# Graph attention over edges on one core: turned one-hots from streamed destination numbers, the other one-hots on GpSimd, eight groups per loop turn

## What is computed

```python
# logx: (H=4, n, DH=64); s_i, s_j: (n, 4)
alpha = leaky_relu(s_i[dst] + s_j[src], 0.2)
m     = segment_max(alpha, dst)
a     = exp(alpha - m[dst])
ssum  = segment_sum(a, dst)                  # a is later divided by ssum[dst]
out   = segment_sum(logx[:, src] * a, dst)   # per head, 64 features
```

## Time and profile before

| | |
|---|---|
| time, median of 3 runs | 9486.06 us (9477.93 to 9505.69) |
| the profiled execution's own time | 9485.6 us |
| its span | 9483.6 us |
| busy: PE, DVE, ACT, POOL | 43%, 42%, 19%, 54% |
| the stretch of `attend`'s groups | about 6972 to 7942 us of the span |

### The profile page before, as it was taken

One profiled execution on the slowest core, in us unless ns is written; L12 is line 12 of the kernel. 1 busy time (PEld: TensorE's weight loads), 2 busy tenths in 40 slices (PEclk: granted clock), 3 DMA queues, 4 the chain that ended last, 5 costly groups with the idle time before them and its releaser, 6 DMA issues. The chain is left out here.

```text
span 9483.6 us, 78659 instructions
## 1 busy us (share of the span) xinstructions
PE 4045.1 (43%) x14501; PEld 2859.4 (30%) x14502; DVE 3947.4 (42%) x8209; ACT 1803.0 (19%) x6789; POOL 5163.3 (54%) x5240
## 2 busy tenths in 40 slices
PE   4000035555476676875454410000046663845444
PEld 2000024444355555433333300000034552333332
DVE  5000023333355555432222367777776666222223
ACT  0000001111100000220000014444446663100000
POOL 5777756666666666126666407777721110166665
PEclk7555567677788888986666655555578887967666
DMA  3000012222255555233333315555553333333334
GB/s 101 3 14 6 3 61 87 88 87 88 102 173 172 171 174 172 48 140 91 92 91 90 71 49 179 180 179 177 178 124 113 115 113 92 134 89 92 91 90 86
DMA packets 390541, 997.00 MB, mean 105 GB/s; under 512 B 133180, under 2 KB 167648, under 8 KB 383836
## 3 DMA queue, kind: packets, MB, share of 16 engines
q0 software_dynamic: 227264, 559.12, 21.0%
q1 hardware_dynamic: 163228, 437.33, 14.0%
HBM read 684.30 MB, written 311.78 MB: 105 GB/s over the span
## 5 line engine op out<-in xcount | busy, mean ns | idle before, releaser
L797 POOL DMA_INDIRECT rel_rows<-relation_rows,rel_ring_row x1664 | 1612.8, 969 | 1400.0 <-ACT rel_ring_end L781 903.2
L809 PE MATMUL rel_sums<-rel_rows,rel_hot 128*128 128x256 f32 x3328 | 1199.9, 505 | 1235.8 <-issue 705.5
L809 PEld LDWEIGHTS rel_sums<-rel_rows,rel_hot 128*128 128x128 f32 x3328 | 817.1, 253 | 1619.5 <-issue 1428.7
L1635 POOL DMA_INDIRECT nmax_rows<-messages,nmax_ring_row x832 | 878.2, 1056 | 653.6 <-ACT nmax_ring_row L1582 393.4
L621 POOL DMA_INDIRECT rows_by_src<-spread_rows,spread_ring_place x832 | 814.0, 978 | 488.3 <-issue 244.6
L694 POOL DMA_INDIRECT both_rows<-batch_normed,both_ring_row x832 | 816.6, 982 | 458.6 <-issue 232.7
L488 POOL DMA_INDIRECT records_by_dst<-sort_ring_rec,sort_ring_place x784 | 836.5, 1067 | 293.1 <-issue 234.5
L599 PE MATMUL spread_p_r<-g_big,spread_hot_t 128*128 x1664 | 632.0, 546 | 561.5 <-ACT spread_hot_t L543 397.7
L833 DVE TENSOR_TENSOR g_acc<-rel_sums,g_acc 128x256 f32 x832 | 351.2, 422 | 1209.1 <-remote 581.8
L706 PE MATMUL both_out_sums<-both_out_rows,both_out_hot 128*128 128x257 f32 x1664 | 515.8, 465 | 405.0 <-DVEq L743 378.4
L1818 PE MATMUL att_sums<-att_weighted,att_hot 128*128 128x260 f32 x1664 | 542.3, 482 | 312.4 <-DVE att_weighted L1888 169.9
(11 more groups left out here) (384 smaller groups left out, 6784.1 us busy)
## 6 DMA issues: line engine op xcount, KB each, us to landing
both_out_rows<-rows_by_src SPq DMA_DIRECT2D x208, 520.0 KB
kept_rows<-nmax_rows SPq DMA_DIRECT2D x208, 520.0 KB
att_rows<-kept_rows SPq DMA_DIRECT2D x208, 520.0 KB
rel_rows<-relation_rows,rel_ring_row POOLq DMA_INDIRECT x1664
relation_rows<-mix_table SPq DMA_DIRECT2D x25, 1024.0 KB
relation_rows<-rel_table SPq DMA_DIRECT2D x25, 1024.0 KB
rows_by_src<-spread_rows,spread_ring_place POOLq DMA_INDIRECT x832
both_rows<-batch_normed,both_ring_row POOLq DMA_INDIRECT x832
```

The costliest lines, as they stand in the source:

```text
L797: pool.indirect_dma_start(rows[:, j, 0:words], None, table, bass.IndirectOffsetOnAxis(ap=ring_row[:, j:j + 1], axis=0)).then_inc(landed[r] ...
L809: last = nc.tensor.matmul(sums[:, 2 * r + q // 2, 0:width], hot[:, j, :], rows[:, j, :], start=q % 2 == 0, stop=q % 2 == 1)
L1635: pool.indirect_dma_start(rows[:, j, :], None, msg_dram.ap(), bass.IndirectOffsetOnAxis(ap=ring_row[:, j:j + 1], axis=0)).then_inc(landed[ ...
```

## The change

1. The local numbers of all edges are also written to DRAM in edge order, as bf16 (`local_of_edge`, 832 x 128). `neighbour_max` makes them before its loop: seven transposes on PE, three copies on ACT, two small stores on SP.
2. `attend` streams them back to all partitions: one DMA puts the 2048 numbers of 16 columns (four groups) on each of the 128 partitions, 512 KB. VectorE compares the whole of it with the partition's own number (`g.own`): one instruction, 128x2048 in bf16, gives the turned one-hots of four groups. The transposes on PE, the copies on ACT and the bf16 one-hots are gone.
3. GpSimd makes the float32 one-hots itself: four comparisons of 128x128 per group, `g.iota` against the edge's number, 832 in all, written out without a loop. The only wait is that the sums of group n-4 are done.
4. A loop turn has eight groups (TURN = 8), so 26 turns; each loads 16 tile numbers at once where it loaded 8.

```diff
+            stream_locals(0, 0)
             for r in range(RING):
                 stream(0, r)
+            stream_locals(0, 1)
...
+            with sp.Fori(1, TURNS) as i:
+                for r in range(TURN):
+                    if r % RING == 1:
+                        sp.wait_ge(turned_ready, i * 2 + (r // RING - 1))
+                        stream_locals(i, r // RING)
+                    sp.wait_ge(ready, i * TURN + (r + 1 - RING))
+                    sp.wait_ge(shared, i * TURN + (r + 1 - RING))
                     stream(i, r)
```

```diff
+            def stream_locals(i, u):
+                sp.dma_start(local_row[:, u, :], local_at[bass.ds(i * (2 * WIDE * P) + u * (WIDE * P), WIDE * P)]
+                             .partition_broadcast(P)).then_inc(local_in[u], 16)
```

```diff
-                nc.gpsimd.tensor_copy(hot[:, s, :], hot_b[:, s, :]).then_inc(widened, 1)
...
+            for n in range(CH // GRP):
+                pool.wait_ge(summed, n + 1)
+                for q in range(GRP):
+                    last = nc.gpsimd.tensor_scalar(hot[:, n % RING * GRP + q, :], g.iota[:],
+                                                   g.rec[0][:, n * GRP + q, 2:3], None, ALU.is_equal)
+                last.then_inc(hot_ready, 1)
```

```diff
+            def build(i, u):
+                dve.wait_ge(local_in[u % 2], (i + u // 2) * 16 + 16)
+                nc.vector.tensor_scalar(hot_t[:, u % 2, :], local_row[:, u % 2, :], g.own[:], None,
+                                        ALU.is_equal).then_inc(turned_ready, 1)
...
-                    if not (last_turn and r == RING - 1):
-                        more = not (last_turn and r >= RING - 3)
-                        scores(i, r + 1, (lambda: build(i, r + 3)) if more else None)
+                    if not (last_turn and r == TURN - 1):
+                        scores(i, r + 1)
+                    if r % RING == 0 and not (last_turn and r == RING):
+                        build(i, r // RING + 1)
                     if not (first and r == 0):
                         before = tiles[2 * r:2 * r + 2]
```

More of the change, by code:

```diff
@@ L1639, in _ @@
         def _(pe):
+            for k in range(STRIPS):
+                count = min(P, CH - k * P)
+                last = nc.tensor.transpose(p_l[0:count, k, :], g.rec[0][:, k * P:k * P + count, 2], g.ident[:])
+            last.then_inc(local_turn, 1)
             for t in range(T):
@@ L1720, in attend @@
         sums = m.ps("sums", [P, 4, 512])
-        p_t = m.ps("p_t", [P, 2, 2 * GRP, P], BF16)
         p_s = m.ps("p_s", [P, 2, 512])
-        (tick, shared, hot_ready, widened, turn, back, looked, alphas, exps, ready, summed, added, vec, psum_free) = (
-            m.sem(n) for n in ("tick", "shared", "hot_ready", "widened", "turn", "back", "looked", "alphas", "exps", "ready",
+        (shared, hot_ready, turned_ready, looked, alphas, exps, ready, summed, added, vec, psum_free) = (
+            m.sem(n) for n in ("shared", "hot_ready", "turned_ready", "looked", "alphas", "exps", "ready",
                                "summed", "added", "vec", "psum_free"))
         landed = [m.sem(f"landed_{r}") for r in range(RING)]
+        local_in = [m.sem(f"local_in_{u}") for u in range(2)]
         own_in = m.sem("own_in")
@@ L1749, in _ @@
         def _(pool):
[L1750 to L1759 removed]
+            for n in range(CH // GRP):
[4 more added lines that the diff above has]
+                last.then_inc(hot_ready, 1)
         @block.scalar
         def _(act):
[L1763 to L1773 removed]
+            with act.Fori(0, TURNS) as i:
+                for r in range(TURN):
+                    at = r % RING * GRP
+                    act.wait_ge(alphas, i * TURN + (r + 1))
+                    act.wait_ge(summed, i * TURN + (r + 1))
+                    nc.scalar.activation(weighted[:, at:at + GRP, D:W], alpha[:, r % 2, :, :],
                                          ACT.Exp).then_inc(exps, 1)
[L1775 to L1776 removed]
+                    act.wait_ge(exps, i * TURN + (r + 1))
+                    for q in range(at + GRP - SHARE, at + GRP):
                         for h in range(H):
@@ L1863, in then @@
                     c.wait()
-                c.step(nc.vector.tensor_reduce(
+                then(nc.vector.tensor_reduce(
                     seen[:].rearrange("p q s -> p (q s)"),
                     p_s[:, r % 2, 0:PARTS * GRP].rearrange("p (s n) -> p s n", n=3), AX.X, ALU.add))
-                if more:
-                    more()
-                c.wait()
                 then(nc.vector.tensor_tensor(al, rows[:, at:at + GRP, D:W], seen[:, :, 0:H], ALU.add))
@@ L2048, in build @@
         hyperbolic_prepare(nc, g, a, lx_dram, msg_dram)
-        neighbour_max(nc, g, msg_dram, kept_dram)
+        neighbour_max(nc, g, msg_dram, kept_dram, local_dram)
         clear(nc, (g.acc[:],))
-        attend(nc, g, kept_dram, msg_dram)
+        attend(nc, g, kept_dram, local_dram, msg_dram)
         hyperbolic_finish(nc, g, a, o_dram)
```

158 lines of the change are left out of this document (71 added, 87 removed).

## The result

The changed kernel takes 9575.4 us (median of 4 runs, 9567.47 to 9582.93), the kernel before 9488.84 (4 runs, 9477.93 to 9505.69): ratio 1.0086, 95% interval 1.007 to 1.0102, so 66 to 97 us slower. The profiled execution took 9567.47 us, its span is 9565.5.

What follows compares the result with a forecast made beforehand. A chain of waits, not one engine, was taken to bound `attend`. The terms summed to 20.52 us per four groups, 1059 us for the stage against 970, plus 3 before the loop: 9578 us, range 9468 to 9690.

Steps and rivals of the forecast that it cites:

- four groups: DVE's chain in `attend`: a group falls from 3.91 to 3.10 us, so four take 12.40.
- GpSimd beside DVE: GpSimd's comparisons, about 0.30 us each, delay DVE by one instruction per meeting: 1.10 us per four groups.
- wait and wide comparison: DVE's wait for the streamed numbers, 3.80 us, plus its wide comparison, 0.80 us, per four groups.
- TensorE's clock: After idling during the wait, PE runs its next sums slowly and delays the look-up: 1.20 us per four groups.
- loop turn: Half as many turns, with sixteen tile numbers costing no more than eight: 1.22 us per four groups, from 2.45.
- The scores get shorter: On DVE, alpha's first step starts 0.48 us sooner and its last step is 0.33 us shorter, per group.
- The wide comparison: DVE's bf16 comparison of 2048 elements per partition takes 0.80 us, bounds 0.70 and 2.3.
- The wait: Numbers issued behind rows on SP land 4.65 us after the multiplications' end; DVE waits 3.80 us, 50 times.
- rival 2: The streamed numbers land before DVE needs them, so no wait: 838 us for `attend`, 9357 in all; chance 0.09.
- rival 1: The wait stays, GpSimd costs nothing: 9521 us, or 9474 if the DMA also overlaps better; chance 0.27.
- rival 3: DVE stays blocked through all four GpSimd comparisons, 2.6 us for 1.10 per four groups: 9656 us; chance 0.18.

Runs made afterwards that it cites:

- e1_early: The changed kernel with the streamed numbers for each wide comparison issued four groups earlier on SP; 8482.95 us, ratio 0.985 to the kernel before.
- e7_quarter: e1_early with one of GpSimd's four comparisons per group (all four in the first four groups only); ratio 0.982 to the kernel before.
- e3_poolcmp: The kernel before with only GpSimd's copy replaced by the four float32 comparisons; 8569.86 us, ratio 0.9949.
- e5_spread: e1_early with tile numbers loaded two at a time, behind the multiplications on VectorE and ahead of each look on TensorE; 9180.47 us, ratio 0.9756.
- e10_plain: The kernel before with GpSimd's copy replaced by four comparisons and tile numbers loaded two at a time, without streamed numbers; 8487.46 us, ratio 0.9859.

## Why the prediction was right, and where two errors cancelled

Direction, size (+87 us measured, +92 predicted) and the central mechanism held. Per four groups, the turn printed above gives 40.71 / 2 = 20.36 us against 20.52. The terms:

| term | predicted | measured |
|---|---|---|
| four groups | 12.40 | 12.40 (taken over) |
| GpSimd beside DVE | 1.10 | 0.35 |
| wait and wide comparison | 3.80 + 0.80 | 4.59 |
| TensorE's clock | 1.20 | 0.91 |
| loop turn | 1.22 | 2.12 |
| sum | 20.52 | 20.37 |

"Measured" comes from the rows of the timeline: the turn is 4.37 less the 0.14 of an ordinary place, halved; the clock is (0.94 + 0.87) / 2; wait and comparison are the time from the end of alpha to the additions, 7500.36 to 7505.37, less the 0.41 gap that stands there in other groups (4.60, and 4.58 for the second). What is left of 40.71 is 25.49, or 12.75 per four groups; 12.40 is taken as forecast and 0.35 given to GpSimd. That is an upper limit: by the instructions that get longer beside GpSimd in the changed kernel's trace (139 multiplications by 21 ns, 130 last steps of alpha by 36, 26 wide comparisons by 66) it is 9 us, 0.2 per four groups.

- **The scores get shorter: right.** The first step of alpha starts 0.28 us behind the reduction, and the last takes 0.17 to 0.23; undisturbed groups take 3.11 to 3.14.
- **The wide comparison: right**, 753 ns by the median of its 52, 786 by the mean. It is nearer to my 0.80 than to the Trainium skill's 693 ns ("VectorE: DVE Perf Modes", "The perf-mode tier table"), which it exceeds by 60.
- **The wait: right in kind, a little short.** Rows issued at m + 0.17 (m = 7499.57), numbers 0.52 behind them, data on the way until about 7504.2 = m + 4.6, as forecast. The comparison starts only at m + 5.09: some 0.5 us pass after the last data. It comes 50 times in the loop, as forecast. e1_early shows that the wait, and not the comparison or the bytes, is what the change lost by. The prediction's rival 2, the numbers in time, gave 838 us for the stage; e1_early's stretch is 813.
- **TensorE's clock: right**, 0.9 in place of 1.2: sums at 3.81 and 3.70 behind each wait, then the look-up is late by 0.94 and 0.87.
- **The loop turn: wrong.** The step that failed is "sixteen tile numbers per load cost no more than eight, by the loop that already loads 16". The gap grew from 2.59 to 4.37, so halving the turns saved 131.5 - 110.0 = 21.5 us, not 64. What went wrong is told below: the row came from a loop whose load of 16 is a cheaper one, 0.42 us in the very turn of the earlier trace rows, against 3.60 here.
- **GpSimd beside DVE: wrong twice, in opposite directions.** The comparison was estimated at 0.30 us from a select; it takes 0.60 (median). The meeting with DVE was priced as a full wait for one instruction, by the copy's example; e7_quarter shows 19 us for three quarters of them, and in e3_poolcmp alpha's last step is not held at all. The size of the term is at most 0.35 and not 1.10, 39 us over the stage.

The two errors, 0.90 too little and 0.75 too much, cancelled by luck; without it the forecast would have been off by some 40 to 47 us, still within the range. Rivals 1 and 3 asked what GpSimd costs: rival 1, with nothing, was nearer to it than the forecast, and still gave too low a time, 9521, since its loop turn was as wrong.

The rule behind rival 3 stands on the page "SBUF — State Buffer", section "Who interferes with whom" of the Trainium skill: whoever issues first has the shared ports for a whole instruction. It describes the copy (0.50 us in place of 0.18), and not these comparisons, which take 600 ns: the step of alpha stays at 175 ns beside them in e3_poolcmp, and where it is held, in e1_early, it takes 231 ns by the median and 286 at most. The measurement decides here. Why the copy holds DVE to its end, and a comparison only for a small part of its time, no run here shows.

## What to carry to other kernels

When a new transfer feeds a step on the critical engine, look for the instruction in whose shadow it is issued: here it stood in the queue behind a wait that is met when the engine already wants the data, and the same transfer issued four groups earlier turned a loss of 0.9% into a gain of 1.5%. Price loads of registers by their own rows, and not by the gap of another loop, and put them behind running work in small pieces: worth 75 to 82 us of the stretch in each of the three kernels in which it was tried (against 964.3 on chip A for the kernel before). And count idle time on TensorE twice: behind its idle time of 3.8 us the sums of the next group took 3.81 us, where they take 1.99 at full clock.

## What the runs showed of the hardware

**Loads of tile numbers.** The profile has a row for them, which the prediction did not read. First the changed kernel in `attend`, 16 numbers (by line: count, then ns as min/median/max; DVEq and PEldq are the engines' sequencers):

```profile
L928 PEldq TENSOR_LOAD <-g_pair_tile x27: 555/3805/3835, 6961.0 to 7984.0; - x27
L928 DVEq TENSOR_LOAD <-g_pair_tile x27: 525/3604/3622, 6968.6 to 8020.0; - x27
```

The kernel before in three stages: `neighbour_max` (8 numbers from 8 i on), `attend` (8 from 8 i - 2 on), and the second `aggregate` (16 from 16 i on):

```profile
L926 DVEq TENSOR_LOAD <-g_pair_tile x61: 594/606/1721, 5007.8 to 6911.2; - x61
...
L926 DVEq TENSOR_LOAD <-g_pair_tile x53: 526/1845/1849, 6973.2 to 7939.9; - x53
...
L926 DVEq TENSOR_LOAD <-g_pair_tile x26: 5/1097/1114, 8233.9 to 9426.9; - x26
```

and e5_spread, 2 numbers:

```profile
L928 PEldq TENSOR_LOAD <-g_pair_tile x208: 532/537/570, 6890.7 to 7631.5; - x104
L928 DVEq TENSOR_LOAD <-g_pair_tile x208: 523/529/549, 6901.9 to 7638.4; - x104
```

In `attend`, 2, 8 and 16 numbers take 0.53, 1.85 and 3.60 us: 0.22 us for each more. The Trainium skill ("Runtime: NRT & Kernel Launch", "Instruction fetch mechanics") puts a load of registers at about 200 ns for each, speaking of those that the runtime puts in; the rows of `attend` come near it. The other two stages don't: 8 numbers take 0.60 us there and 16 take 1.10, a third as long. The loop of the earlier trace rows, the first `aggregate`, has such loads too; in the turn from which the failed step of the prediction was read it took 0.42 us:

```profile
L926 DVEq TENSOR_LOAD <-g_pair_tile x1: 418/418/418, 4723.7 to 4723.7; - x1
```

The visible difference is where the first number stands, at a multiple of the count or two off it. TensorE's loads in an early stage (1289 to 2454 us of the span) fit this: 24 numbers from 24 i on, 1.74 us by the median of 17, where 16 take it 3.80 in `attend`. That this is the cause is a guess, and was not tried.

**The queue runs ahead.** A load of 0.53 us behind two multiplications leaves next to no gap on DVE (e5_spread): with 208 of them in place of 26 loads of 3.60 us, the idle time ahead of the multiplications falls by 95 us, and that ahead of the reduction stays at 14.9, with 1.0 of "issue".

**GpSimd.** A comparison with a number per partition, 128x128 in float32, takes 590 ns at least, twice a select of that size; the four of one group, at 7503.57, took 2.84 us. Beside DVE both sides pay a little: in e1_early the 286 multiplications that start while a comparison runs take 450 ns by the median, the 110 that meet none 422; and the 117 comparisons that meet multiplications, the reduction and the first steps of alpha take 867 ns by the median, where 600 is usual. No step of alpha beside a comparison took longer than 343 ns (in e3_poolcmp, e1_early, e5_spread and e10_plain), while the copy to float32, 617 ns mean, held the last step to 497.

**Data and semaphore.** Behind two DMAs of 520 and 512 KB the waiting instruction starts about 0.5 us after the last slice with data, at both waits of the turn shown.
